# Routed expert tiles: fp16 halves turned one tile later, and router logits with the tokens stationary

## The chip, the core and the metric

One core of a Trainium2 chip runs the whole program. The metric is device time in microseconds (us), median of three runs. Engines: PE is the matrix engine (TensorE; PEld its weight loads), DVE VectorE, ACT ScalarE, POOL GpSimd, SP the engine that only issues transfers.

## The reference

Four layers work in sequence on x (8 x 256 tokens, 512 features): cross attention, a ternary feed-forward layer, linear cross attention, and a mixture of experts. The change touches only the last:

```python
g = x @ sw1.T
u = x @ sw2.T
shared_out = jax.nn.silu(g) * u @ sw3.T                      # 2048 hidden
scores = jax.nn.sigmoid(x @ router_w.T)                      # 8 experts
_, top_idx = jax.lax.top_k(scores + expert_bias, TOPK)       # TOPK = 2
...
h12 = jnp.einsum('td,ehd->teh', flat_x, w12)                 # h1, h2: 256 each
h = jax.nn.silu(h1) * h2
out_e = jnp.einsum('teh,edh->ted', h, w3)
routed_out = jnp.einsum('ted,te->td', out_e, combine)
return shared_out + routed_out
```

## The kernel before

Phases A, B and C are the first three layers; phase D (`phase_d`) is the mixture of experts. Precision comes from fp16 pairs: each fp32 operand is a high fp16 half and a low one (the rest), and a product is three matmuls, high x high, high x low, low x high (helper `three`, lines 140 to 142).

**Shared expert.** Eight chunks of 256 hidden features, four blocks of 512 tokens, two halves of a chunk: 64 steps s. In step s PE does gate(s), up(s), down(s-1), 12 matmuls of 512 columns each. ACT and DVE make SiLU times up (`d_hid`) and its halves (`d_hh`, `d_hl`). Steps 56 to 63, the last chunk, stand behind the routed tiles.

**Router logits.** In steps 1, 3, 5 and 7 `logits(t)` does one block of 512 tokens: the router weights (`r_wT`, 16 columns, high and low halves of 8 experts; `r_wZ`, high and zeros) are stationary and the tokens move, 8 matmuls (L2426, L2427) into 16 partitions of bank 6. ACT copies that to `r_lgT` (L2576), and a step later `logits_turned` turns it back, four fp32 transposes (L2435) into bank 7. DVE's `add_logits` reads the result in step 9.

**Routed tiles.** Tokens are sorted into NT = 39 tiles of 128, each of one expert, whose number stands in `owner`. For tile j:
- POOL gathers the rows of its tokens into `e_x` (L2396, a ring of GR = 3). It waits until both transposes of tile j-3 have landed.
- SP turns both halves by DMA into `e_xTh` and `e_xTl` (L2357, L2358), again a ring of three.
- PE `routed_up(j)`: 12 matmuls of 512 columns, bank 6 or 7. ACT takes SiLU (L2543), DVE multiplies (L2699), into fp32 `d_hid`.
- PE `routed_turn(j)`: two fp32 transposes (L2476) into bank 0 or 1. ACT takes the high half to `d_hh` (L2549), DVE the low one to `d_hl` (L2704).
- PE `routed_down(j)`: 6 matmuls of 512 columns, bank 4 or 5. ACT copies the result to `e_y` (L2555) and SP stores it to `made` (L2361).

PE's order is up(j), down(j-1), turn(j). Before up and before down PE's sequencer loads the expert's number from `owner` into a register (L2457), from which the weights' addresses are made. Behind the last tile come gate(56), down(38), up(56), with waits for the copies of tiles 37 and 38, because banks 4 and 5 serve both.

SP's order, which the change leaves alone, is a single loop:

```python
for j in range(NT + 3):
    if j < NT:
        sp.wait_ge(g_in[j % GR], 16 * (j // GR) + 16)
        if j >= GR:
            sp.wait_ge(e_u, j - GR + 1)
        sp.dma_start_transpose(eTh[:, j % GR], xg[:, j % GR, 0, :])...
        sp.dma_start_transpose(eTl[:, j % GR], xg[:, j % GR, 1, :])...
    if j >= 3:
        sp.wait_ge(e_y, j - 2)
        sp.dma_start(made[(j - 3) * P:(j - 2) * P, :], y[:, (j - 3) % YR, :])...
```

`e_y` at j - 2 means that tiles 0 to j-3 have been copied. So the transposes of tile k are issued behind the store of tile k-4. Afterwards POOL gathers the finished rows back (L2403) and DVE adds them to X (L2681).

Of the kernel before, what the change touches and what calls it, by code (L numbers as in the profile page):

```python
# [15 lines left out]
F32 = mybir.dt.float32  # L16
# [2097 lines left out]
def phase_d(nc, a, env):  # L2114

    sem, bank, X, ident, tg, three = (env[k] for k in ("sem", "bank", "X", "ident", "tg", "three"))
# [3 lines left out]
    def sb(name, shape, dt=F32, stack=None):  # L2120
# [36 lines left out]
    rwZ = sb("r_wZ", [P, KC, 2 * E], F16, rst)  # L2157
    lgT = sb("r_lgT", [2 * E, 2, BLK], F32, rst)
# [31 lines left out]
    w3l = sb("e_w3l", [P, E, KC, HC, P], F16)  # L2190
    y, YR = env["y"], 2
# [7 lines left out]
    r_in, r_wt, r_whi, r_wlo, r_lg, r_lt, r_turn, r_add, r_sig, r_ch, r_cst, r_one, r_msk, r_cnt, r_cut, r_hot, r_used, \  # L2199
        r_who, r_done = (sem("r_" + n) for n in (  # L2200
            "in", "wt", "whi", "wlo", "lg", "ltaken", "turned", "add", "sig", "ch", "const", "ones", "chosen",
# [8 lines left out]
    EUP, EDN, ETH = 6, 4, 0  # L2210
    e_tr = sem("e_turned")
# [47 lines left out]
    def pe_gate(pe, s):  # L2259
        c, t, j = s // SPC, s // JC % BPC, s % JC  # L2260
        if s > 1:
            pe.wait_ge(d_s, s)
        for k in range(KC):
            last = three(bank[GATE][:, :], whs[:, c % 2, 0, k, j * P:(j + 1) * P], wls[:, c % 2, 0, k, j * P:(j + 1) * P],
                         XTh[:, k, t * BLK:(t + 1) * BLK], XTl[:, k, t * BLK:(t + 1) * BLK], k == 0, k == KC - 1)
        last.then_inc(d_g, 1)

    def pe_up(pe, s):
        c, t, j = s // SPC, s // JC % BPC, s % JC
        if s > 1:  # L2270
            pe.wait_ge(d_hm, s)
        for k in range(KC):
            last = three(bank[UP][:, :], whs[:, c % 2, 1, k, j * P:(j + 1) * P], wls[:, c % 2, 1, k, j * P:(j + 1) * P],
                         XTh[:, k, t * BLK:(t + 1) * BLK], XTl[:, k, t * BLK:(t + 1) * BLK], k == 0, k == KC - 1)
        last.then_inc(d_u, 1)
# [15 lines left out]
    def act_step(act, s):  # L2291
        act.wait_ge(d_g, s + 1)
        if s >= 2:
            act.wait_ge(d_lo, s - 1)
        nc.scalar.activation(hid[:, s % 2, :], bank[GATE if s else 0][:, :], ACT.Silu).then_inc(d_s, 1)  # L2295
        act.wait_ge(d_hm, s + 1)
        if s >= 2:
            act.wait_ge(d_dn, s - 1)
        nc.scalar.activation(hh[:, s % 2, :], hid[:, s % 2, :], ACT.Copy).then_inc(d_hi, 1)  # L2299

    def dve_hid(dve, s):
        dve.wait_ge(d_u, s + 1)
        dve.wait_ge(d_s, s + 1)
        nc.vector.tensor_tensor(hid[:, s % 2, :], hid[:, s % 2, :], bank[UP if s else 1][:, :], ALU.mult).then_inc(d_hm, 1)  # L2304
# [22 lines left out]
    with nc.Block() as block:  # L2327
# [80 lines left out]
        def _(pe):  # L2408
# [11 lines left out]
            def logits(t):  # L2420
                pe.wait_ge(r_wlo, 1)
                if t:
                    pe.wait_ge(r_lt, t)
                for k in range(KC):
                    cols = slice(t * BLK, (t + 1) * BLK)
                    nc.tensor.matmul(bank[LG][0:2 * E, :], rwT[:, k, :], XTh[:, k, cols], start=(k == 0), stop=False)  # L2426
                    last = nc.tensor.matmul(bank[LG][0:2 * E, :], rwZ[:, k, :], XTl[:, k, cols], start=False,  # L2427
                                            stop=(k == KC - 1))
                last.then_inc(r_lg, 1)

            def logits_turned(t):
                pe.wait_ge(r_lt, t + 1)
                for i in range(TPB):
                    c = (TILES + t * TPB + i) * 2 * E
                    last = nc.tensor.transpose(bank[TR][:, c:c + 2 * E], lgT[:, t % 2, i * P:(i + 1) * P],  # L2435
                                               ident[0:2 * E, 0:2 * E])
                last.then_inc(r_turn, 1)
# [21 lines left out]
            def routed_up(j):  # L2459
                e = expert(j)  # L2460
                pe.wait_ge(g_tp[j % GR], 32 * (j // GR) + 32)
                if j >= 2:
                    pe.wait_ge(e_m, j - 1)
                for k in range(KC):
                    hi = w12h[:, bass.ds(e, 1), k, :].rearrange("p o c -> p (o c)")
                    lo = w12l[:, bass.ds(e, 1), k, :].rearrange("p o c -> p (o c)")
                    last = three(bank[EUP + j % 2][:, :], eTh[:, j % GR, k, :], eTl[:, j % GR, k, :], hi, lo,
                                 k == 0, k == KC - 1)
                last.then_inc(e_u, 1)

            def routed_turn(j):
                pe.wait_ge(e_m, j + 1)
                if j >= 2:
                    pe.wait_ge(e_lo, j - 1)
                for k in range(HC):
                    last = nc.tensor.transpose(bank[ETH + j % 2][:, k * P:(k + 1) * P], hid[:, j % 2, k * P:(k + 1) * P],  # L2476
                                               ident[:, :])
                last.then_inc(e_tr, 1)

            def routed_down(j):  # L2480
                e = expert(j)
                pe.wait_ge(e_lo, j + 1)
                if j >= 2:
                    pe.wait_ge(e_y, j - 1)
                for k in range(HC):
                    hi = w3h[:, bass.ds(e, 1), :, k, :].rearrange("p o r c -> p (o r) c")
                    lo = w3l[:, bass.ds(e, 1), :, k, :].rearrange("p o r c -> p (o r) c")
                    cols = slice(k * P, (k + 1) * P)
                    last = three(bank[EDN + (j + 1) % 2][:, :].rearrange("p (r c) -> p r c", r=KC), hh[:, j % 2, cols],
                                 hl[:, j % 2, cols], hi, lo, k == 0, k == HC - 1)  # L2490
                last.then_inc(e_dn, 1)

            for s in range(NS * SPC):
                if s == LAST * SPC:
                    pe_down(pe, s - 1)
                    pe.wait_ge(r_done, 2)
                    pieces_turned(pe, NQ - 1)
                    for j in range(NT):
                        routed_up(j)
                        if j:  # L2500
                            routed_down(j - 1)
                        else:
                            pe.wait_ge(d_acc, LAST * BPC)
                        routed_turn(j)
                    pe.wait_ge(e_y, NT - 1)
                    pe_gate(pe, s)
# [19 lines left out]
                if s and s <= SPC and s % JC == 0:  # L2526
                    logits_turned(s // JC - 1)
# [8 lines left out]
        def _(act):  # L2536
            env["ln_normal"](act, "d", B - 1)

            def routed_silu(j):
                act.wait_ge(e_u, j + 1)  # L2540
                if j >= 2:
                    act.wait_ge(e_tr, j - 1)
# [14 lines left out]
            for s in range(NS * SPC):  # L2557
                if s == LAST * SPC:
                    act.wait_ge(d_dn, s)
                    for j in range(NT):  # L2560
                        routed_silu(j)
                        if j:
                            routed_result(j - 1)
                        routed_high(j)
# [6 lines left out]
                if s < SPC and s % JC == JC - 1:  # L2571
                    t = s // JC
                    act.wait_ge(r_lg, t + 1)
                    if t >= 2:
                        act.wait_ge(r_turn, t - 1)
                    nc.scalar.activation(lgT[:, t % 2, :], bank[LG][0:2 * E, :], ACT.Copy).then_inc(r_lt, 1)  # L2576
# [5 lines left out]
        def _(dve):  # L2582
# [4 lines left out]
            def add_logits():  # L2587
                dve.wait_ge(r_turn, BPC)
# [113 lines left out]
            def routed_low(j):  # L2702
                dve.wait_ge(e_hi, j + 1)
                nc.vector.tensor_tensor(hl[:, j % 2, 0:FR], bank[ETH + j % 2][:, 0:FR], hh[:, j % 2, 0:FR],  # L2704
                                        ALU.subtract).then_inc(e_lo, 1)

            def router():
                dve.wait_ge(r_in, 32)
                dve.wait_ge(r_whi, 1)
                link(nc.vector.tensor_tensor(rwT[:, :, E:2 * E], bank[TR][:, 0:KC * E].rearrange("p (k e) -> p k e", k=KC),  # L2710
                                             rwT[:, :, 0:E], ALU.subtract))
                nc.vector.memset(rwZ[:, :, E:2 * E], 0.0)
                nc.vector.tensor_copy(rwZ[:, :, 0:E], rwT[:, :, 0:E]).then_inc(r_wlo, 1)
# [5 lines left out]
            for s in range(NS * SPC):  # L2719
                if s == LAST * SPC:  # L2720
                    dve_result(dve, s // JC - 1)
                    for j in range(NT):
                        routed_mul(j)
                        routed_low(j)
                dve_hid(dve, s)
# [71 lines left out]
```

## Time and profile before

| | us |
|---|---|
| median of three runs (lowest to highest) | 1724.37 (1722.57 to 1724.7) |
| span of the profiled execution | 1722.0 |
| its time over the span | the median less the span is 2.4 |
| first routed up matmul to first matmul of up(56) | 1471.1 to 1655.2 |
| router logits, first to last matmul | 1036.5 to 1092.0 |

The profiled execution's own time is taken as the median, 2.4 us over its span. In a timeline a matmul's length includes the way through the array (0.38 us for 512 columns), while the next begins 0.215 us later; "idle" counts from the end so drawn.

### The profile page before, as it was taken

How to read it: one execution, taken by the hardware profiler on the slowest of the kernel's cores; microseconds unless marked ns; L12 is line 12 of the kernel's file. 1: busy time of each engine (PE TensorE's matmuls, PEld its weight loads, DVE VectorE, ACT ScalarE, POOL GpSimd, SP SyncE). 2: the span in 40 equal slices, each digit the busy share in tenths (PEclk: the TensorE clock that was granted, in tenths of full speed). 3: DMA queues.
4: the chain of work that ended last, by engine and by line, in shares of the span. 5: the costliest groups of instructions: out<-in, count | busy, mean ns of one | idle time of the engine just before them, and what ended most of it. 6: DMA issues, size and time to landing. Idle time of an engine off the chain costs nothing. (4 is left out here: it accounts for less than half of the span.)

```text
span 1722.0 us, 29300 instructions
## 1 busy us (share of the span) xinstructions
PE 1587.8 (92%) x10826; PEld 829.3 (48%) x10826; DVE 973.1 (57%) x1947; ACT 709.2 (41%) x1311; POOL 824.3 (48%) x853
## 2 busy tenths in 40 slices
PE   5769999999877999899999989999999999999998
PEld 3336665665443444345656544444444444444443
DVE  5736666778736999845665543377454333211146
ACT  3268888888855655532232321211111111222221
POOL 3478887877853545443452434344333532112134
PEclk9989999999878999999999999999999999999999
DMA  6745444322333555444554426447454754477746
GB/s 182 160 102 112 99 106 109 93 67 72 92 73 84 110 119 114 93 86 86 96 120 95 78 74 156 110 105 153 92 101 101 154 101 95 109 173 172 168 138 195
DMA packets 453955, 195.68 MB, mean 114 GB/s; under 512 B 395500, under 2 KB 418286, under 8 KB 453816
## 3 DMA queue, kind: packets, MB, share of 16 engines
q1 hardware_dynamic: 448136, 175.19, 46.0%
q0 software_dynamic: 5680, 18.62, 4.1%
q8 instruction: 89, 1.46, 0.4%
q14 instruction: 50, 0.41, 0.1%
HBM read 77.17 MB, written 22.81 MB: 58 GB/s over the span
## 5 line engine op out<-in xcount | busy, mean ns | idle before, releaser
L1109 POOL TENSOR_TENSOR a_pl<-a_prob,a_ph 128x512 f16<-128x512 f32 x256 | 295.2, 1166 | 72.7 <-ACT a_prob L996 72.3
L1199 DVE TENSOR_REDUCE a_mx<-bank 128x2 f32<-128x512 f32 x256 | 173.3, 686 | 97.1 <-PE bank L690 95.5
L140 PE MATMUL bank<-XTh,d_whs 128*128 128x512 f16 x512 | 194.9, 381 | 4.2 <-PEq L89 2.4
L141 PE MATMUL bank<-XTl,d_whs 128*128 128x512 f16 x512 | 194.7, 380 | 0.0
L142 PE MATMUL bank<-XTh,d_wls 128*128 128x512 f16 x512 | 194.6, 380 | 0.0
L995 ACT ACTIVATE a_ph<-bank 128x512 f16<-128x512 f32 x256 | 153.9, 601 | 73.3 <-PE bank L710 35.9
L2384 POOL CAST d_cut<-d_raw 128x512 f16<-128x512 f32 x90 | 56.2, 624 | 227.7 <-DMA d_raw<-in_L_ffn_sw 146.8
L996 ACT ACTIVATE a_prob<-bank 128x512 f32<-128x512 f32 x256 | 154.4, 603 | 0.0
L2304 DVE TENSOR_TENSOR d_hid<-d_hid,bank 128x512 f32<-128x512 f32 x64 | 43.9, 686 | 172.1 <-PE bank L142 168.2
L2295 ACT ACTIVATE d_hid<-bank 128x512 f32<-128x512 f32 x64 | 38.2, 597 | 204.7 <-PE bank L142 204.7
L2299 ACT ACTIVATE d_hh<-d_hid 128x512 f16<-128x512 f32 x64 | 40.3, 630 | 194.7 <-DVE d_hid L2304 194.7
L727 PE MATMUL bank<-a_v,a_ph 128*128 128x17 f16 x1024 | 103.8, 172 | 16.9 <-POOL a_pl L1109 16.9
L2396 POOL DMA_INDIRECT e_x<-rows,d_who x39 | 37.2, 955 | 164.2 <-DMA e_xTl<-e_x 158.1
L2386 POOL TENSOR_TENSOR d_cut<-d_raw,d_cut 128x512 f16<-128x512 f32 x90 | 107.2, 1191 | 7.2
L1502 PE MATMUL bank<-b_wpj,b_hTh 128*128 128x512 f16 x256 | 99.6, 389 | 12.0 <-DMA b_hTl<-b_hcut 12.0
L727 PEld LDWEIGHTS bank<-a_v,a_ph 128*128 128x128 f16 x1024 | 89.0, 97 | 40.1 <-POOL a_pl L1109 18.6
L710 PE MATMUL bank<-a_qT,a_kT 128*128 128x512 f16 x256 | 101.3, 396 | 7.4 <-ACT a_prob L996 7.4
L690 PE MATMUL bank<-a_kT,a_qT 128*128 128x256 f16 x512 | 98.5, 275 | 7.0 <-DVE a_mx L1199 6.6
L2314 DVE SCALAR_TENSOR_TENSOR X<-bank,tg,X 128x512 f32<-128x512 f32 x112 | 76.3, 744 | 49.9 <-PE bank L142 49.9
L731 PE MATMUL bank<-a_v,a_pl 128*128 128x17 f16 x1024 | 102.3, 171 | 0.0
L729 PE MATMUL bank<-a_v,a_ph 128*128 128x16 f16 x1024 | 102.1, 170 | 0.0
L1503 PE MATMUL bank<-b_wpj,b_hTl 128*128 128x512 f16 x256 | 99.4, 388 | 0.0
(349 smaller groups left out, 3996.4 us busy)
## 6 DMA issues: line engine op xcount, KB each, us to landing
d_raw<-in_L_ffn_w SPq DMA_DIRECT2D x48, 256.0 KB, 3.1
d_raw<-in_L_ffn_sw SPq DMA_DIRECT2D x42, 256.0 KB, 3.1
made<-e_y SPq DMA_DIRECT2D x39, 256.0 KB
a_stage<-in_L_ffn_w_fc SPq DMA_DIRECT2D x32, 256.0 KB, 2.9
a_stage<-in_L_ffn_w_proj SPq DMA_DIRECT2D x32, 256.0 KB, 3.1
a_fbuf<-in_ctx SPq DMA_DIRECT2D x16, 256.0 KB, 3.5
rows<-f_cut SPq DMA_DIRECT2D x16, 256.0 KB, 2.5
out_x<-X SPq DMA_DIRECT2D x16, 256.0 KB, 2.4
```

Of the source, the lines that this page charges most:

```text
L140: nc.tensor.matmul(out_ap, lhi, rhi, start=first, stop=False)
L141: nc.tensor.matmul(out_ap, lhi, rlo, start=False, stop=False)
L142: return nc.tensor.matmul(out_ap, llo, rhi, start=False, stop=last_one)
L710: nc.tensor.matmul(bk[:, :], kT[:, par, 2 * g + half, kc * P:(kc + 1) * P], qT[:, par, 2 * g:2 * g + 2, :].rearrange("p r q -> p (r q)"), ...
L727: nc.tensor.matmul(into[:, c:c + HD0 + 1], ph[:, n % NP, q], vv[:, b % 3, kc, g, 0:HD0 + 1], start=first, stop=False, skip_group_check=True)
L729: nc.tensor.matmul(into[:, c:c + HD0], ph[:, n % NP, q], vv[:, b % 3, kc, g, HD0 + 1:VW], start=False, stop=False, skip_group_check=True)
L731: last = nc.tensor.matmul(into[:, c:c + HD0 + 1], pl[:, n % NP, q], vv[:, b % 3, kc, g, 0:HD0 + 1], start=False, stop=(kc == 1), skip_grou ...
L995: nc.scalar.activation(ph[:, n % NP, :], bank[BST + n % 2][:, :], ACT.Exp)
L996: nc.scalar.activation(prob[:, n % 2, :], bank[BST + n % 2][:, :], ACT.Exp).then_inc(ev["E"], 1)
L1109: nc.gpsimd.tensor_tensor(pl[:, n % NP, :], prob[:, n % 2, :], ph[:, n % NP, :], ALU.subtract).then_inc(ev["L"], 1)
L1199: nc.vector.tensor_reduce(mx[:, h, tt, half, 2 * (g % 4):2 * (g % 4) + 2], bank[BS + m % 2][:, :].rearrange("p (r k) -> p r k", r=2), AX_X ...
L2386: nc.gpsimd.tensor_tensor(cut[:, i % RING, 1, :], raw[:, i % RING, :], cut[:, i % RING, 0, :], ALU.subtract).then_inc(p_lo, 1)
```

## The change

Routed tiles: ACT now takes the high half of the product straight from `d_hid` in SBUF to a new fp16 tile `e_hs`, DVE the low half, and PE turns both: four fp16 transposes, high to bank 0 or 1, low to bank 2 or 3, in place of two fp32 ones. ACT and DVE then copy the turned halves to `d_hh` and `d_hl`. PE's order becomes up(j), down(j-2), turn(j-1). The expert's number is loaded once per tile, behind up, and kept for down. Step 56 uses banks 7 and 6 in place of 4 and 5, and the wait for the last copy moves to step 57.

Router: the tokens are stationary (128 of them), the weights move. 16 tiles of 128 tokens times 8 matmuls of 16 or 8 columns, straight into the layout that `add_logits` reads; `r_wZ`, `r_lgT`, ACT's copies and the fp32 transposes go.

```diff
             def logits(t):
-                pe.wait_ge(r_wlo, 1)
-                if t:
-                    pe.wait_ge(r_lt, t)
-                for k in range(KC):
-                    cols = slice(t * BLK, (t + 1) * BLK)
-                    nc.tensor.matmul(bank[LG][0:2 * E, :], rwT[:, k, :], XTh[:, k, cols], start=(k == 0), stop=False)
-                    last = nc.tensor.matmul(bank[LG][0:2 * E, :], rwZ[:, k, :], XTl[:, k, cols], start=False,
-                                            stop=(k == KC - 1))
+                if t == 0:
+                    pe.wait_ge(r_wlo, 1)
+                for n in range(t * TPB, (t + 1) * TPB):
+                    dst = bank[TR][:, (TILES + n) * 2 * E:(TILES + n + 1) * 2 * E]
+                    cols = slice(n * P, (n + 1) * P)
+                    for k in range(KC):
+                        nc.tensor.matmul(dst, XTh[:, k, cols], rwT[:, k, :], start=(k == 0), stop=False)
+                        last = nc.tensor.matmul(dst[:, 0:E], XTl[:, k, cols], rwT[:, k, 0:E], start=False,
+                                                stop=(k == KC - 1))
                 last.then_inc(r_lg, 1)
...
             def routed_turn(j):
-                pe.wait_ge(e_m, j + 1)
+                pe.wait_ge(e_lo, j + 1)
                 if j >= 2:
-                    pe.wait_ge(e_lo, j - 1)
-                for k in range(HC):
-                    last = nc.tensor.transpose(bank[ETH + j % 2][:, k * P:(k + 1) * P], hid[:, j % 2, k * P:(k + 1) * P],
-                                               ident[:, :])
+                    pe.wait_ge(e_th, j - 1)
+                    pe.wait_ge(e_tl, j - 1)
+                for low in range(2):
+                    for k in range(HC):
+                        last = nc.tensor.transpose(bank16(ETH[low] + j % 2)[:, k * P:(k + 1) * P], hs[:, j % 2, low, k * P:(k + 1) * P],
+                                                   ident16[:, :])
                 last.then_inc(e_tr, 1)
...
+                    owners = {0: expert(0)}
                     for j in range(NT):
-                        routed_up(j)
+                        routed_up(j, owners[j])
+                        if j + 1 < NT:
+                            owners[j + 1] = expert(j + 1)
+                        if j >= 2:
+                            routed_down(j - 2, owners[j - 2])
+                        elif j:
+                            pe.wait_ge(d_acc, LAST * BPC)
                         if j:
-                            routed_down(j - 1)
-                        else:
-                            pe.wait_ge(d_acc, LAST * BPC)
-                        routed_turn(j)
-                    pe.wait_ge(e_y, NT - 1)
+                            routed_turn(j - 1)
+                    routed_down(NT - 2, owners[NT - 2])
+                    routed_turn(NT - 1)
+                    pe.wait_ge(e_m, NT)
                     pe_gate(pe, s)
-                    routed_down(NT - 1)
-                    pe.wait_ge(e_y, NT)
+                    routed_down(NT - 1, owners[NT - 1])
                     pe_up(pe, s)
                     continue
+                elif s == EXPERTS + 1:
+                    pe.wait_ge(e_y, NT)
...
             def routed_high(j):
+                act.wait_ge(e_m, j + 1)
+                if j >= 2:
+                    act.wait_ge(e_tr, j - 1)
+                nc.scalar.activation(hs[:, j % 2, 0, :], hid[:, j % 2, 0:FR], ACT.Copy).then_inc(e_hi, 1)
+
+            def take_high(j):
                 act.wait_ge(e_tr, j + 1)
                 if j >= 2:
                     act.wait_ge(e_dn, j - 1)
-                nc.scalar.activation(hh[:, j % 2, 0:FR], bank[ETH + j % 2][:, 0:FR], ACT.Copy).then_inc(e_hi, 1)
+                nc.scalar.activation(hh[:, j % 2, 0:FR], bank16(ETH[0] + j % 2)[:, 0:FR], ACT.Copy).then_inc(e_th, 1)
...
                     for j in range(NT):
                         routed_silu(j)
+                        routed_high(j)
+                        if j >= 2:
+                            routed_result(j - 2)
                         if j:
-                            routed_result(j - 1)
-                        routed_high(j)
+                            take_high(j - 1)
```

On PE in the routed tiles, before, from the end of a down to the next up (`ident,d_hid` is the fp32 transpose, TENSOR_LOAD with its two ISA rows the read of the expert's number, the third ISA the first address):

```order
L142 MATMUL bank5<-e_w3h,d_hl 128x512
L2476 MATMUL bank1<-ident,d_hid 128x128 x2
L2457 TENSOR_LOAD d_owner
L2457 ISA x2
L140 ISA
L140 MATMUL bank6<-e_w12h,e_xTh 128x512
```

The same place after, from the end of up (bank 6) through down (bank 5) to the next up (bank 7); the repeats inside down are the same five rows for the second half:

```order
L142 MATMUL bank6<-e_w12h,e_xTl 128x512
L2452 TENSOR_LOAD d_owner
L2452 ISA x2
L140 ISA
L140 MATMUL bank5<-e_w3h,d_hh 128x512
```

```order
L142 MATMUL bank5<-e_w3h,d_hl 128x512
L2472 MATMUL bank1<-ident16,e_hs 128x128 x2
L2472 MATMUL bank3<-ident16,e_hs 128x128 x2
L140 ISA
L140 MATMUL bank7<-e_w12h,e_xTh 128x512
```

The load has gone from between transposes and up to between up and down, and down is of a tile two back.

On ACT in the routed tiles, before:

```order
L2543 ACTIVATE d_hid<-bank6 128x256
L2555 ACTIVATE e_y<-bank4 128x512
L2549 ACTIVATE d_hh<-bank0 128x256
L2543 ACTIVATE d_hid<-bank7 128x256
L2555 ACTIVATE e_y<-bank5 128x512
```

And after:

```order
L2544 ACTIVATE d_hid<-bank6 128x256
L2550 ACTIVATE e_hs<-d_hid 128x256
L2562 ACTIVATE e_y<-bank5 128x512
L2556 ACTIVATE d_hh<-bank1 128x256
L2544 ACTIVATE d_hid<-bank7 128x256
```

One instruction more per tile stands ahead of the copy to `e_y`, which is now of the tile two behind the SiLU above it.

## Rows read from the trace of the kernel before

**Rows 1.** The page: busy time, share of span, instructions of each engine.
```profile
PE 1587.8 (92%) x10826; PEld 829.3 (48%) x10826; DVE 973.1 (57%) x1947; ACT 709.2 (41%) x1311; POOL 824.3 (48%) x853
```
**Rows 2.** Waits between 1475 and 1655 us: engine, line, releaser; us, times, longest.
```profile
PE bank L140 <- issue: 12.2, 38, 0.6
```
**Rows 3.** Timeline of one routed tile, start us, us, engine; transfers and copies with it.
```profile
1521.96 0.39 PE L140 MATMUL bank<-e_w12h,e_xTh 128*128 x1 [0.35 <-issue]
...
1524.76 0.38 ACT L2543 ACTIVATE d_hid<-bank 128x256 f32<-128x256 f32 x1 [2.46 <-PE bank L142]
...
1525.17 0.42 DVE L2699 TENSOR_TENSOR d_hid<-d_hid,bank 128x256 f32<-128x256 f32 x1 [2.42 <-ACT d_hid L2543]
...
1525.64 0.38 PE L142 MATMUL bank<-e_w3h,d_hl 128*128 x1
...
1525.85 0.38 PE L2476 MATMUL bank<-ident,d_hid 128*128 128x128 f32 x2
1526.05 0.60 ACT L2555 ACTIVATE e_y<-bank 128x512 f32<-128x512 f32 x1 [0.91 <-PE bank L142]
...
1526.51 0.39 PE L140 MATMUL bank<-e_w12h,e_xTh 128*128 x1 [0.27 <-issue]
...
1526.68 0.32 SPq L2361 DMA_DIRECT2D made<-e_y  x1
...
1527.10 1.22 SPq L2357 DMA_TRANSPOSE e_xTh<-e_x  x1
...
1528.36 1.27 SPq L2358 DMA_TRANSPOSE e_xTl<-e_x  x1
```
**Rows 4.** Timeline of PE: first matmul of the first routed up, first of up(56).
```profile
1471.08 0.38 PE L140 MATMUL bank<-e_w12h,e_xTh 128*128 x1
...
1655.22 0.39 PE L140 MATMUL bank<-XTh,d_whs 128*128 128x512 f16 x1 [0.69 <-ACT e_y L2555]
```
**Rows 5.** Transfers writing e_xTl, last line of the tile's view.
```profile
DMA to landing us min/median/max: 2.5/3.7/5.9
```
**Rows 6.** Timeline of SP and POOL: a low transpose, and the gather it releases; then one more gather.
```profile
1475.14 1.27 SPq L2358 DMA_TRANSPOSE e_xTl<-e_x  x1
...
1477.89 0.94 POOL L2396 DMA_INDIRECT e_x<-rows,d_who  x1 [29.74 <-DMA e_xTl<-e_x]
...
1532.30 0.94 POOL L2396 DMA_INDIRECT e_x<-rows,d_who  x1 [3.41 <-DMA e_xTl<-e_x]
```
**Rows 7.** Timeline of PE: logits of one block, and its transposes, with neighbours.
```profile
1036.23 0.38 PE L142 MATMUL bank<-d_whd,d_hl 128*128 128x512 f16 x1
1036.54 0.38 PE L2426 MATMUL bank<-XTh,r_wT 128*16 128x512 f16 x1
...
1038.37 0.39 PE L140 MATMUL bank<-XTh,d_whs 128*128 128x512 f16 x1
...
1045.93 0.38 PE L142 MATMUL bank<-d_whd,d_hl 128*128 128x512 f16 x1
1046.24 0.42 PE L2435 MATMUL bank<-ident,r_lgT 16*128 16x16 f32 x4
1046.59 0.39 PE L140 MATMUL bank<-XTh,d_whs 128*128 128x512 f16 x1
```
**Rows 8.** Phase A: twelve short matmuls with loads between them, first and next matmul.
```profile
111.82 0.17 PE L727 MATMUL bank<-a_v,a_ph 128*128 128x17 f16 x1
...
112.12 0.38 PE L687 MATMUL bank<-a_madd,ident 128*128 128x512 f16 x1
```
**Rows 9.** Phase A by line: weight loads (ns min/median/max), eight fp16 transposes (start, us).
```profile
L727 PEld LDWEIGHTS bank<-a_v,a_ph x1024: 95/96/152, 79.3 to 504.2; 128*128 128x128 f16 x171
...
67.00 0.61 PE L673 MATMUL bank<-ident,a_ks 128*128 128x128 f16 x8
```
**Rows 10.** Stretches: length, busy PE, PEld, DVE, ACT, POOL; granted clock, DMA share, GB/s.
```profile
430.00:473.00 43.00, 35.20 (x447) 21.09 (x445) 33.59 (x64) 36.85 (x72) 37.72 (x36) 0.84 0.36 90
...
1471.00:1655.00 184.00, 169.74 (x794) 80.21 (x791) 35.71 (x82) 48.90 (x117) 31.17 (x33) 1.00 0.65 154
```

More of the change, by code:

```diff
@@ L2114, in phase_d @@
 def phase_d(nc, a, env):
-    sem, bank, X, ident, tg, three = (env[k] for k in ("sem", "bank", "X", "ident", "tg", "three"))
+    sem, bank, bank16, X, ident, ident16, tg, three = (env[k] for k in (
+        "sem", "bank", "bank16", "X", "ident", "ident16", "tg", "three"))
     XTh, XTl, whs, wls, whd, wld, rows = (env[k] for k in ("XTh", "XTl", "whs", "wls", "whd", "wld", "rows"))
@@ L2156, in phase_d @@
     rwT = sb("r_wT", [P, KC, 2 * E], F16, rst)
-    rwZ = sb("r_wZ", [P, KC, 2 * E], F16, rst)
-    lgT = sb("r_lgT", [2 * E, 2, BLK], F32, rst)
     ebias = sb("r_bias", [P, E], F32, rst)
@@ L2190, in phase_d @@
     w3l = sb("e_w3l", [P, E, KC, HC, P], F16)
+    hs = sb("e_hs", [P, 2, 2, FR], F16)
     y, YR = env["y"], 2
@@ L2198, in phase_d @@
     p_hi, p_lo = sem("p_hi"), sem("p_lo")
-    r_in, r_wt, r_whi, r_wlo, r_lg, r_lt, r_turn, r_add, r_sig, r_ch, r_cst, r_one, r_msk, r_cnt, r_cut, r_hot, r_used, \
+    r_in, r_wt, r_whi, r_wlo, r_lg, r_add, r_sig, r_ch, r_cst, r_one, r_msk, r_cnt, r_cut, r_hot, r_used, \
         r_who, r_done = (sem("r_" + n) for n in (
-            "in", "wt", "whi", "wlo", "lg", "ltaken", "turned", "add", "sig", "ch", "const", "ones", "chosen",
+            "in", "wt", "whi", "wlo", "lg", "add", "sig", "ch", "const", "ones", "chosen",
             "counts", "cut", "hot", "used", "who", "done"))
@@ L2209, in phase_d @@
     GATE, UP, LG, TR = 4, 5, 6, 7
-    EUP, EDN, ETH = 6, 4, 0
-    e_tr = sem("e_turned")
+    EUP, EDN, ETH = 6, 4, (0, 2)
+    e_tr, e_th, e_tl = (sem("e_" + n) for n in ("turned", "taken_hi", "taken_lo"))
+    EXPERTS = LAST * SPC
+    GATE_OF, UP_OF = {0: 0, EXPERTS: 7}, {0: 1, EXPERTS: 6}
     ROUND = 12582912.0
@@ L2263, in pe_gate @@
         for k in range(KC):
-            last = three(bank[GATE][:, :], whs[:, c % 2, 0, k, j * P:(j + 1) * P], wls[:, c % 2, 0, k, j * P:(j + 1) * P],
+            last = three(bank[GATE_OF.get(s, GATE)][:, :], whs[:, c % 2, 0, k, j * P:(j + 1) * P], wls[:, c % 2, 0, k, j * P:(j + 1) * P],
                          XTh[:, k, t * BLK:(t + 1) * BLK], XTl[:, k, t * BLK:(t + 1) * BLK], k == 0, k == KC - 1)
@@ L2272, in pe_up @@
         for k in range(KC):
-            last = three(bank[UP][:, :], whs[:, c % 2, 1, k, j * P:(j + 1) * P], wls[:, c % 2, 1, k, j * P:(j + 1) * P],
+            last = three(bank[UP_OF.get(s, UP)][:, :], whs[:, c % 2, 1, k, j * P:(j + 1) * P], wls[:, c % 2, 1, k, j * P:(j + 1) * P],
                          XTh[:, k, t * BLK:(t + 1) * BLK], XTl[:, k, t * BLK:(t + 1) * BLK], k == 0, k == KC - 1)
@@ L2294, in act_step @@
             act.wait_ge(d_lo, s - 1)
-        nc.scalar.activation(hid[:, s % 2, :], bank[GATE if s else 0][:, :], ACT.Silu).then_inc(d_s, 1)
+        nc.scalar.activation(hid[:, s % 2, :], bank[GATE_OF.get(s, GATE)][:, :], ACT.Silu).then_inc(d_s, 1)
         act.wait_ge(d_hm, s + 1)
@@ L2303, in dve_hid @@
         dve.wait_ge(d_s, s + 1)
-        nc.vector.tensor_tensor(hid[:, s % 2, :], hid[:, s % 2, :], bank[UP if s else 1][:, :], ALU.mult).then_inc(d_hm, 1)
+        nc.vector.tensor_tensor(hid[:, s % 2, :], hid[:, s % 2, :], bank[UP_OF.get(s, UP)][:, :], ALU.mult).then_inc(d_hm, 1)
     def dve_low(dve, s):
@@ L2420, in logits @@
             def logits(t):
-                pe.wait_ge(r_wlo, 1)
-                if t:
-                    pe.wait_ge(r_lt, t)
-                for k in range(KC):
-                    cols = slice(t * BLK, (t + 1) * BLK)
-                    nc.tensor.matmul(bank[LG][0:2 * E, :], rwT[:, k, :], XTh[:, k, cols], start=(k == 0), stop=False)
-                    last = nc.tensor.matmul(bank[LG][0:2 * E, :], rwZ[:, k, :], XTl[:, k, cols], start=False,
-                                            stop=(k == KC - 1))
-                last.then_inc(r_lg, 1)
[L2431 to L2437, printed above, removed]
+                if t == 0:
[7 more added lines that the diff above has]
+                                                stop=(k == KC - 1))
+                last.then_inc(r_lg, 1)
             def counts():
@@ L2457, in expert, with routed_up @@
                 return pe.value_load(owner[0:1, j:j + 1], min_val=0, max_val=E - 1)
-            def routed_up(j):
-                e = expert(j)
+            def routed_up(j, e):
                 pe.wait_ge(g_tp[j % GR], 32 * (j // GR) + 32)
@@ L2471, in routed_turn, with routed_down @@
             def routed_turn(j):
-                pe.wait_ge(e_m, j + 1)
+                pe.wait_ge(e_lo, j + 1)
                 if j >= 2:
-                    pe.wait_ge(e_lo, j - 1)
-                for k in range(HC):
-                    last = nc.tensor.transpose(bank[ETH + j % 2][:, k * P:(k + 1) * P], hid[:, j % 2, k * P:(k + 1) * P],
-                                               ident[:, :])
+                    pe.wait_ge(e_th, j - 1)
[4 more added lines that the diff above has]
+                                                   ident16[:, :])
                 last.then_inc(e_tr, 1)
-            def routed_down(j):
-                e = expert(j)
-                pe.wait_ge(e_lo, j + 1)
+            def routed_down(j, e):
+                pe.wait_ge(e_th, j + 1)
+                pe.wait_ge(e_tl, j + 1)
                 if j >= 2:
@@ L2525, in _ @@
                     logits(s // JC)
-                if s and s <= SPC and s % JC == 0:
-                    logits_turned(s // JC - 1)
                 if s == SPC + 6:
@@ L2541, in routed_silu @@
                 if j >= 2:
-                    act.wait_ge(e_tr, j - 1)
+                    act.wait_ge(e_lo, j - 1)
                 nc.scalar.activation(hid[:, j % 2, 0:FR], bank[EUP + j % 2][:, 0:FR], ACT.Silu).then_inc(e_s, 1)
             def routed_high(j):
+                act.wait_ge(e_m, j + 1)
[3 more added lines that the diff above has]
+            def take_high(j):
                 act.wait_ge(e_tr, j + 1)
@@ L2561, in _ @@
                         routed_silu(j)
+                        routed_high(j)
+                        if j >= 2:
+                            routed_result(j - 2)
                         if j:
-                            routed_result(j - 1)
-                        routed_high(j)
+                            take_high(j - 1)
+                    routed_result(NT - 2)
+                    take_high(NT - 1)
                     routed_result(NT - 1)
@@ L2570, in _ @@
                                          ACT.Copy).then_inc(r_whi, 1)
[L2571 to L2576, printed above, removed]
                 if s == SPC + 1:
@@ L2587, in add_logits @@
             def add_logits():
-                dve.wait_ge(r_turn, BPC)
+                dve.wait_ge(r_lg, BPC)
                 lg = bank[TR][:, TILES * 2 * E:2 * TILES * 2 * E].rearrange("p (t e) -> p t e", t=TILES)
@@ L2703, in routed_low, with take_low @@
                 dve.wait_ge(e_hi, j + 1)
-                nc.vector.tensor_tensor(hl[:, j % 2, 0:FR], bank[ETH + j % 2][:, 0:FR], hh[:, j % 2, 0:FR],
+                nc.vector.tensor_tensor(hs[:, j % 2, 1, :], hid[:, j % 2, 0:FR], hs[:, j % 2, 0, :],
                                         ALU.subtract).then_inc(e_lo, 1)
+            def take_low(j):
+                dve.wait_ge(e_tr, j + 1)
+                if j >= 2:
+                    dve.wait_ge(e_dn, j - 1)
+                nc.vector.tensor_copy(hl[:, j % 2, 0:FR], bank16(ETH[1] + j % 2)[:, 0:FR]).then_inc(e_tl, 1)
             def router():
@@ L2709, in router @@
                 dve.wait_ge(r_whi, 1)
[L2710 to L2713, printed above, removed]
+                nc.vector.tensor_tensor(rwT[:, :, E:2 * E], bank[TR][:, 0:KC * E].rearrange("p (k e) -> p k e", k=KC),
+                                        rwT[:, :, 0:E], ALU.subtract).then_inc(r_wlo, 1)
                 dve.wait_ge(r_cst, 1)
@@ L2724, in _ @@
                         routed_low(j)
+                        if j:
+                            take_low(j - 1)
+                    take_low(NT - 1)
                 dve_hid(dve, s)
```

## The prediction, made before the changed kernel ran

> **What bounds the kernel now.** I read the page first: PE is busy 92% of the span [rows 1]. So a change must take time from PE's stream, or it is paid for nothing. Then the timeline of one routed tile [rows 3]: up begins at 1521.96 and the last of 18 wide matmuls at 1525.64, 17 steps of 0.2165 us, so 18 take 3.9. The fp32 transposes follow at 1525.85 without a gap and hold PE for some 0.21 (the pair is drawn 0.38 long, of which 0.17 is the way through the array). The next up comes only at 1526.51, so PE stands 0.66 - 0.21 = 0.45 us. The view of waits calls that "issue", 38 times, 12.2 us (plus 0.17 each that is drawn as busy) [rows 2]. Its place explains it: PE's sequencer stands at the transposes for DVE's product, ready at 1525.17 + 0.42 = 1525.59 [rows 3], and only then reads the next expert's number from memory. The same read ahead of down costs nothing, since PE still has matmuls queued. A tile takes 4.55 us, and the whole stretch from the first up to up(56) 1655.22 - 1471.08 = 184.1 [rows 4].
>
> Last I looked at who feeds the tiles. SP's store of a result starts at 1526.68, the transpose of the high half at 1527.10, of the low one at 1528.36 [rows 3]. No PE wait names a transfer now. The question is how much room there is.
>
> **Routed tiles, PE's own work.** Removed: two fp32 transposes of 0.21 together and the 0.45 stall. Added: four fp16 transposes. Eight of these are drawn 0.61 long in phase A [rows 9]; less 0.17 that is 0.055 each, so four take 0.22, no gain. The read of the number now stands behind up with 12 wide matmuls queued, the place that is free today. If PE alone set the pace, a tile would take 3.9 + 0.22 = 4.1, and 39 tiles plus the 12 matmuls of gate(56), 2.6, take 162.9 in place of 184.1: minus 21.2. That includes the waits at the first tile and around gate(56), for which the change has cover (another up, other banks).
>
> **Routed tiles, the loop through SP.** Count from u(j), the start of up(j). Up and the down behind it run without a gap, the copy to `e_y` starts at 1526.05, so u + 4.09; the store at u + 4.72, the high transpose at u + 5.14, the low one at u + 6.40 [rows 3]. The low one lands a median of 3.7 later [rows 5]. POOL's gather, which waits for that landing, starts 3.94 behind the low transpose of 1528.36 [rows 3, 6]; I take the same 3.9 for PE, landing and wake together. So the transposed tile is ready at 6.4 + 3.9 = 10.3 us past the up that stands before the down whose result was stored.
>
> SP issues the transposes of tile k behind the store of tile k-4. Before, down(k-4) follows up(k-3): tile k is ready at u(k-3) + 10.3 and wanted at u(k-3) + 3 x 4.55 = 13.65, 3.3 us in hand. After, down(k-4) follows up(k-2). Tile k is ready at u(k-2) + 10.3 and wanted two tiles on, at 8.2 by PE's pace, even at today's pace only 9.1. The change spends a whole tile of lead that it doesn't give back at SP. Hence u(k) = u(k-2) + 10.3, 5.15 us a tile.
>
> The sum: up(0), up(1), a turn, then u(2) = 5.4, u(4) = 5.4 + 10.3 = 15.7, and 17 round trips to u(38) = 15.7 + 17 x 10.3 = 190.8. Behind it up, down, turn, down, turn, gate, down: 2.6 + 1.3 + 0.2 + 1.3 + 0.2 + 2.6 + 1.3 = 9.5. Total 200.3 against 184.1, so **plus 16.2**.
>
> Bounds of the landing with its wake: 2.75, the first gather in rows 6 (1475.14 to 1477.89, no other gather in flight); and 4.4, some way over the median toward the 5.9 of rows 5. With 2.75 the loop is 9.15: u(4) = 14.55, u(38) = 170.1, total 179.6, minus 4.5. With 4.4 it is 10.8: 199.8, 209.3, plus 25.2. I take 3.9 because after the change a gather again starts about when a tile's up starts, so beside the next transposes, as in the second case of rows 6.
>
> The Trainium skill, page "DMA: Bandwidth & Descriptors", section "Anatomy of one DMA — SWDGE (gpsimd) path", fits a transfer as about 2.0 us plus bytes over 436 GB/s; as an estimate a 128 KB half would then need 2.3. By that the loop is 8.9 with the wake, and the stretch falls by 9.0. The trace disagrees: the least is 2.5 and the median 3.7 [rows 5].
>
> Engines on the loop: ACT takes the high half ahead of the copy. It can start at 1525.59 + 0.06 and takes between 0.38 (the SiLU of the same 256 columns) and 0.60 (the copy of 512) [rows 3]; with 0.40, near its equal in size, it ends at u + 4.09, just as the copy can start. Taken at nothing; at 0.60 the loop grows by 0.2 and the sum by 3.5. ACT's four instructions sum to under 2 us, DVE's three to 1.3, both within 4.1, and the turned halves are wanted a whole up later, so neither waits.
>
> **Router logits.** One block: from 1036.23 + 0.22 to 1038.37, 1.92; its four fp32 transposes with their edges from 1045.93 + 0.22 to 1046.59, 0.44 [rows 7]. Four blocks: 9.4 us of PE. After: 32 matmuls per block with a full load before each and 16 or 8 columns. Phase A has that shape: twelve in 112.12 - 111.82 = 0.30, 0.025 each [rows 8], although a load is drawn 96 ns long [rows 9]. So 32 x 0.025 + 0.2 for the edges = 1.0 a block, 4.0 in all: **minus 5.4**. Bounds: if a burst of 32 ran at the 0.055 of the fp16 transposes, 7.8, minus 1.6; if each load stood unhidden, 4 x (32 x 0.096 + 0.2) = 13.1, plus 3.7. I take 0.025, the same shape. PE is the chain here, and SP's weight loads wait for PE's downs, so the gain passes on. ACT's four copies, two DVE instructions and a tile of zeros go as well: nothing, since neither engine holds PE there.
>
> The Trainium skill, page "TensorE: Matmul & The Clock Gate", section "LDWEIGHTS (loading the stationary operand)", says that a load takes its columns over 1.2 ns, which speaks against this edit: 107 ns for 128 columns, by estimate 14.5 us for the four blocks, plus 5.1. The trace agrees on the length of one (96) and not that it sets the pace (25).
>
> **Sum.** 16.2 - 5.4 = plus 10.8. The last chunk's own work is unchanged. Up(56) no longer waits for the last copy, 0.69 us plus the 0.17 drawn as busy [rows 4], so POOL's gathers back of the results begin some 0.9 later against PE; that costs between nothing and 0.9, and I take nothing, since a step of the last chunk has 7.8 us of matmuls over DVE's additions. On the median that is 1724.4 + 10.8 = 1735.2.
>
> **Rivals.**
> - *The transposes land sooner* (faster). SP's loop holds, but with a longer tile the gather, store and transposes meet less; DMA share is 0.65 in the stretch [rows 10]. Landing with wake of 2.75 gives minus 4.5 - 5.4, so 1714.5; the total is below the old one while that term is under 3.3. For it: the first case of rows 6. Against: all tiles in a row are fed beside a gather. Between 3.1 and 3.5 the kernel lands within 3.4 us of the old time. The estimate from the Trainium skill's page above would end at 1710.
> - *PE sets the pace after all* (faster). If SP's order doesn't bind, minus 21.2 - 5.4: 1698. Against it stands SP's code order: only a landing and wake under 8.2 - 6.4 = 1.8 allows it, below every row.
> - *Loads set the logits.* Plus 3.7 in place of minus 5.4: 1744.
> - *The clock falls.* PE would be busy 4.1 of 5.15, 80%. In phase A a stretch with 35.2 of 43, 82%, had a granted clock of 0.84 against 1.00 here [rows 10], a mean of time at 2.4 and at 1.2 GHz. At 0.84 up and down take 0.75 more, the loop 11.05: 17 x 0.75 = 12.8 more, 1748.
>
> **How the numbers follow.** Forecast with a landing term of 3.5 to 4.4 (1728 to 1744): 0.58. Loads in the logits 0.04, the clock 0.06. The landing between (within 0.2%, 3.4 us, which is about what a measurement of this kernel can tell from no change): 0.12. Sooner 0.14, PE's pace 0.06. Slower 0.58 + 0.04 + 0.06 = 0.68, same 0.12, faster 0.20. The range leaves out PE's pace, the clock and the far ends of the loads and the landing: 1714 to 1744.
>
> **What would show it.** Right: PE's waits for a transfer into `e_xTh` or `e_xTl` ahead of up, 18 or more times, near 2 us per two tiles; "issue" ahead of up gone; results a mean 5.15 apart; the low transpose starting 6.4 behind an up and that up two before the one it feeds; logits blocks of 1.0. Wrong: results 4.1 apart with no such wait; or low transposes landing within 3.1, or logits matmuls 0.05 to 0.1 apart.

## The result

The changed kernel takes 1733.56 us, median of 16 runs (1725.89 to 1737.99). The kernel before, run beside it, takes 1725.31, median of 16 (1722.40 to 1728.63). The ratio is 1.0046, with a 95% interval of 1.0035 to 1.0057: 8.2 us slower.

| | before | after |
|---|---|---|
| span of the profiled execution | 1722.0 | 1731.2 |
| first logits matmul to first routed up | 434.5 | 427.6 |
| first routed up to first matmul of up(56) | 184.1 | 199.9 |
| up(56) to the end | 66.8 | 66.7 |

Two things moved, in opposite directions: the stretch that holds the logits lost 7 us, the routed tiles gained 15.8. (The first logits matmul itself starts 0.5 us later in this profile, 1037.08 against 1036.54, with nothing changed ahead of it.)

### The profile page after: what moved, and what is told of

Its sections match the earlier page's. It is cut to its first block and busy times, and to the rows that moved or that the text cites. A ratio compares the mean times of both kernels' runs of the same rounds, so it can differ in the third digit from the quotient of the medians.

```text
span 1731.2 us, 29642 instructions
## 1 busy us (share of the span) xinstructions
PE 1588.8 (92%) x10984; PEld 833.6 (48%) x10984; DVE 979.2 (57%) x1984; ACT 723.6 (42%) x1346; POOL 824.4 (48%) x853
```

## The profile after

The page's first part. PE is as busy as in [rows 1], 92%, of a longer span:

```profile
span 1731.2 us, 29642 instructions
## 1 busy us (share of the span) xinstructions
PE 1588.8 (92%) x10984; PEld 833.6 (48%) x10984; DVE 979.2 (57%) x1984; ACT 723.6 (42%) x1346; POOL 824.4 (48%) x853
```

The view of PE's waits over the routed tiles (line, releaser; us, times, longest). It answers to [rows 2]:

```profile
PE bank L140 <- DMA e_xTl<-e_x: 28.8, 29, 2.2
PE bank L140 <- ACT d_hh L2556: 0.8, 1, 0.8
```

"Issue" ahead of up has gone. In its place 29 of the 39 ups wait for the transposed low half. With the 0.17 us per wait that are drawn as busy, that is 28.8 + 29 x 0.17 = 33.7 us, against 12.2 + 38 x 0.17 = 18.7 before.

The timeline of one tile and what it sets going, to be laid beside [rows 3]:

```profile
1505.12 0.39 PE L140 MATMUL bank<-e_w12h,e_xTh 128*128 x1
...
1508.33 0.42 DVE L2704 TENSOR_TENSOR d_hid<-d_hid,bank 128x256 f32<-128x256 f32 x1 [2.88 <-ACT d_hid L2544]
...
1508.79 0.42 ACT L2550 ACTIVATE e_hs<-d_hid 128x256 f16<-128x256 f32 x1 [0.49 <-DVE d_hid L2704]
...
1509.01 0.39 PE L2472 MATMUL bank<-ident,e_hs 128*128 128x128 f16 x4
1509.21 0.60 ACT L2562 ACTIVATE e_y<-bank 128x512 f32<-128x512 f32 x1
...
1509.84 0.32 SPq L2363 DMA_DIRECT2D made<-e_y  x1
1510.25 1.22 SPq L2359 DMA_TRANSPOSE e_xTh<-e_x  x1
...
1510.45 0.39 PE L140 MATMUL bank<-e_w12h,e_xTh 128*128 x1 [1.05 <-DMA e_xTl<-e_x]
...
1511.52 1.27 SPq L2360 DMA_TRANSPOSE e_xTl<-e_x  x1
```

Every distance is the one of before: copy at u + 4.09, store at u + 4.72, high transpose at u + 5.13, low one at u + 6.40. ACT's new instruction (0.42) ends at 1509.21, exactly when the copy can start. The up at 1510.45 waits 1.05 + 0.17 us, and what releases it is its own low transpose, issued 3.34 us earlier, at 1507.11:

```profile
1507.11 1.31 SPq L2360 DMA_TRANSPOSE e_xTl<-e_x  x1
```

The transposes issued at 1510.25 and 1511.52 serve the up after that one. The view of the transfers into `e_xTl` ends, in place of [rows 5], with

```profile
DMA to landing us min/median/max: 2.5/3.5/5.7
```

The stretch of the routed tiles (length, busy PE, PEld, DVE, ACT, POOL, granted clock, DMA share, GB/s), beside [rows 10]:

```profile
1464.50:1666.30 201.80, 171.92 (x881) 82.15 (x880) 43.61 (x121) 65.66 (x157) 31.36 (x33) 0.99 0.59 140
```

The transfer engines are less busy than before (0.59 against 0.65), and yet PE waits for them. That points to a latency and not a rate; e1 tests it.

The mean clock of 0.99 hides one place. Behind a wait of 2.07 us one up ran mostly at the lower of PE's two levels, 1.2 GHz (granted clock 0.50 from 1523 to 1525): it took 5.81 us to the next up in place of 4.11, so 1.7 were lost. Its matmuls are drawn 0.63 long in place of 0.38:

```profile
1521.22 0.39 PE L140 MATMUL bank<-e_w12h,e_xTh 128*128 x1 [2.07 <-DMA e_xTl<-e_x]
...
1523.06 0.63 PE L140 MATMUL bank<-e_w12h,e_xTh 128*128 x1
...
1527.03 0.38 PE L140 MATMUL bank<-e_w12h,e_xTh 128*128 x1
```

The logits of one block, beside [rows 7]:

```profile
1036.87 0.38 PE L142 MATMUL bank<-d_whd,d_hl 128*128 128x512 f16 x1
1037.08 0.17 PE L2429 MATMUL bank<-r_wT,XTh 128*128 128x16 f16 x1
1037.11 0.17 PE L2430 MATMUL bank<-r_wT,XTl 128*128 128x8 f16 x1
...
1037.86 0.17 PE L2430 MATMUL bank<-r_wT,XTl 128*128 128x8 f16 x1
1037.89 0.38 PE L140 MATMUL bank<-XTh,d_whs 128*128 128x512 f16 x1
```

32 matmuls in 0.81 us, 25 ns each, and no edge on either side: 0.81 in place of 1.92 + 0.44.

## The experiments

The theory: the changed kernel is bound by the loop through SP's order, in which transposes of tile k wait for the result of tile k-4, and the change took one tile of lead from it. The rivals: the transfer engines are the bound at any order; the new order on PE or the added work on ACT and DVE costs the time; the stall that the change removes is something other than the read of the expert's number.

| kernel | median us | ratio to the kernel before | 95% interval |
|---|---|---|---|
| changed kernel | 1733.56 | 1.0046 | 1.0035 to 1.0057 |
| e1, changed, SP's store one tile later | 1699.34 | 0.985 | 0.9827 to 0.9873 |
| e2, before, router's part only | 1717.28 | 0.9948 | 0.993 to 0.9966 |
| e3, before, routed part only | 1740.17 | 1.0086 | 1.0067 to 1.0106 |
| e4, before, only the number read once and earlier | 1707.77 | 0.9891 | 0.987 to 0.9913 |
| e5, before, SP's store one tile sooner | 1747.15 | 1.0145 | 1.0117 to 1.0173 |
| e6, before, SP's store one tile later | 1724.78 | 1.0008 | 0.9993 to 1.0022 |
| e7, changed, 36 gathers left out | 1719.38 | 0.9964 | 0.995 to 0.9979 |
| e8, e4 and e2 together | 1700.10 | 0.9861 | 0.9835 to 0.9887 |

The kernel before had a median of 1726.41 beside e1 to e4 (11 runs) and 1724.95 over the 19 runs that e5 to e8 are compared with.

### e1: the lead given back at SP

```diff
-            for j in range(NT + 3):
+            for j in range(NT + 4):
...
-                if j >= 3:
-                    sp.wait_ge(e_y, j - 2)
-                    sp.dma_start(made[(j - 3) * P:(j - 2) * P, :], y[:, (j - 3) % YR, :])...
+                if j >= 4:
+                    sp.wait_ge(e_y, j - 3)
+                    sp.dma_start(made[(j - 4) * P:(j - 3) * P, :], y[:, (j - 4) % YR, :])...
```

> The changed kernel with one edit on SP: the store of tile j-4 instead of j-3 stands behind the transposes of tile j, so that the transposes of tile k wait for the result of tile k-5. Theory (the loop through SP's order bounds the changed kernel): a transposed tile is then ready 10.3 us past an up that stands three tiles ahead, and wanted at 3 x 4.1 = 12.3, so PE's waits for e_xTl vanish, results come 4.1 us apart, the stretch from the first routed up to up(56) falls from 199.9 to about 163 and the time to about 1697. Rival (the transfer engines themselves are the bound, whatever the order): they were busy 65% of 4.55 us, 3.0 us per tile, so at 4.1 they would be near 0.73 to 0.8 with landings of 5 us and more; PE's waits for e_xTl stay and the pace stays over 4.6, time over 1715.

Measured: 1699.34 us, 34 less than the changed kernel. PE's waits in the routed tiles, where the changed kernel has 28.8 us for `e_xTl`:

```profile
PE bank L140 <- DMA e_xTl<-e_x: 1.3, 2, 0.8
PE bank L140 <- ACT d_hh L2556: 0.8, 1, 0.8
```

Results come from 1474.1 to 1630.4:

```profile
L2562 ACT ACTIVATE e_y<-bank x39: 597/597/598, 1474.1 to 1630.4; 128x512 f32<-128x512 f32 x39
```

that is 156.3 over 38 intervals, 4.11 a tile. The first routed up to up(56) takes 165.6, against 199.9 in the changed kernel and about 163 expected. The landing has become longer, not shorter:

```profile
DMA to landing us min/median/max: 2.5/3.9/5.9
```

The transfer engines are busy 0.78 of that stretch, against 0.59 in the changed kernel. So the same transfers at a higher rate, landing later, hold PE only twice once there is a tile of lead. That rules out the transfer engines as the bound of the changed kernel.

### e5 and e6: the same edit on the kernel before, in both directions

```diff
-            for j in range(NT + 3):
+            for j in range(NT + 2):
...
-                if j >= 3:
-                    sp.wait_ge(e_y, j - 2)
-                    sp.dma_start(made[(j - 3) * P:(j - 2) * P, :], y[:, (j - 3) % YR, :])...
+                if j >= 2:
+                    sp.wait_ge(e_y, j - 1)
+                    sp.dma_start(made[(j - 2) * P:(j - 1) * P, :], y[:, (j - 2) % YR, :])...
```

> The kernel before, PE's order untouched, with one edit on SP: the store of tile j-2 instead of j-3 stands behind the transposes of tile j. That takes a tile of lead from the transposes without the change's new order. Theory (the lost lead alone makes the loss): the transposed tile is ready 10.3 us past an up only two tiles ahead, PE waits for e_xTl appear, results come some 5.1 us apart, about plus 16 to plus 20 us, near 1744. Rival (the loss comes from the new order on PE or the extra instructions on ACT and DVE): no wait for e_xTl, time as before within 3 us.

Measured: 1747.15, plus 22.2, somewhat more than the 16 to 20 expected (the profiled execution took 1743.71). PE's matmuls, their order and ACT's and DVE's work are those of the kernel before, and the waits of the changed kernel are there:

```profile
PE bank L140 <- DMA e_xTl<-e_x: 26.9, 30, 2.5
PE bank L140 <- issue: 2.5, 8, 0.4
```

Results run from 1481.2 to 1674.6, 5.09 a tile:

```profile
L2555 ACT ACTIVATE e_y<-bank x39: 597/597/598, 1481.2 to 1674.6; 128x512 f32<-128x512 f32 x39
```

From u(4), the start of up(4), to u(38) there are 17 round trips of 10.26 us, where the changed kernel has 10.27. The pace of the slowed kernels is the same whether the tile of lead is taken on SP or on PE. e5 has neither the new order on PE nor the added work on ACT and DVE, so these don't make the loss. The other direction is e1's edit on the kernel before.

> The kernel before with the SP edit of e1_after_more_lead alone (the store of tile j-4 behind the transposes of tile j). Theory (the kernel before has 3.3 us in hand and isn't bound by SP): within 2 us of the kernel before. Rival (part of the gain of e1_after_more_lead is a gain of SP's order in any kernel): faster by over 5 us.

Measured: 1724.78, ratio 1.0008 with an interval that holds 1, as expected. The kernel before had lead in hand; more of it is worth nothing there. So e1's gain is the removal of a bound that the change had brought.

### e4: what the stall of before was

```diff
-            def routed_up(j):
-                e = expert(j)
+            def routed_up(j, e):
...
-            def routed_down(j):
-                e = expert(j)
+            def routed_down(j, e):
...
+                    owners = {0: expert(0)}
                     for j in range(NT):
-                        routed_up(j)
+                        routed_up(j, owners[j])
+                        if j + 1 < NT:
+                            owners[j + 1] = expert(j + 1)
                         if j:
-                            routed_down(j - 1)
+                            routed_down(j - 1, owners[j - 1])
```

The read that stood ahead of down goes too, as in the change: `routed_down` gets the number that was read for its up.

> The kernel before, where only the read of the next tile's expert number moves from between the transposes and up to between up and down; PE's order of the matmuls, the fp32 transposes and SP's order stay. Theory (the 0.45 us stall at each tile is that read behind a stopped sequencer): PE's issue waits ahead of up shrink from 12.2 us (plus 0.17 each drawn as busy) to a few, a tile takes 4.1 to 4.2 us, and the transposed tile, ready 10.3 us past an up three tiles ahead, is still in time for 12.3: minus 13 to minus 17, about 1710. Rival (the stall is the wait for DVE's product and the restart of the sequencer, not the read): the stall stays over 0.3 and the time falls by less than 5. Second rival (feeding binds at that pace): waits for e_xTl appear.

Measured: 1707.77, minus 18.6 against 1726.41, a little more than expected. The same place as in [rows 3], between the fp32 transposes and the next up:

```profile
1522.23 0.38 PE L142 MATMUL bank<-e_w3h,d_hl 128*128 x1
...
1522.44 0.38 PE L2475 MATMUL bank<-ident,d_hid 128*128 128x128 f32 x2
...
1522.66 0.38 PE L140 MATMUL bank<-e_w12h,e_xTh 128*128 x1
```

Up now starts 0.22 us behind the transposes, not 0.66. There is no "issue" row left among PE's waits. The stall was the read of the number in that place: DVE's product and the fp32 transposes still stand where they stood, and the transposes take their own 0.22 us and no more. 38 times 0.44 is 16.7 of the 18.6. The second rival fails as well: no wait for `e_xTl` appears.

### e2 and e3: the two parts apart

e2 is the kernel before with `logits(t)` and what hangs on it as in the change; e3 has all of the rest of the change.

> The kernel before with the router's part of the change alone. Theory (short matmuls 25 ns apart): four blocks shrink from 9.4 to 3.3 us on PE, minus 6 to minus 7 us, about 1718.5. Rival (part of it is lost again where DVE's router chain holds PE, in the steps behind): minus 3 or less.

> The kernel before with the routed tiles' part of the change alone. Theory: the stretch from the first routed up to up(56) grows from 184.1 to about 200, plus 15 to 16 us, about 1741; together with the router's part alone it adds up to the whole change (plus 8). Rival: the parts don't add, since the router's part shifts the gathers of the first tiles against PE; then the sum of the two misses the whole by over 3 us.

Measured: e2 minus 9.1, e3 plus 13.8 against 1726.41, both 1 to 3 us lower than expected. Together plus 4.6, against plus 8.2 for the whole. The difference of 3.6 is a little more than the rival's 3 us. By the ratios of the table it is 2.1 (plus 5.9 against plus 7.9). But the intervals are 6 us wide for e2 and 7 for e3, so the sum doesn't decide. The profiles say more. In e2 the routed stretch begins at 1467.86 and the first logits matmul stands at 1040.44, so 427.4, where the changed kernel has 427.6. In e3 the last up's first matmul can be told from the last of line 140, 1662.8, against the first, 1472.4: 190.4, where the changed kernel has 1655.9 less 1464.6 = 191.3. Within each stretch the parts add to 1 us; I hold the rest to be scatter between runs, which isn't shown.

### e7: what lengthens a landing

POOL gathers only the first three tiles; the rows of the other 36 are left out, and SP doesn't wait for them (its edit isn't shown):

```diff
                 if j >= GR:
-                    pool.wait_ge(g_tp[j % GR], 32 * (j // GR))
+                    continue
                 pool.indirect_dma_start(xg[:, j % GR, :, :]...
```

> The changed kernel with gathers for the first three tiles only; later tiles turn the rows already in the ring, so 36 gathers of 256 KB are left out and their rows are wrong in the output. Theory (a gather beside the transposes lengthens the landing of the low one from about 2.5 to 3.5 us): the landing of e_xTl falls to 2.5 to 2.8 (median), the loop from 10.0 to 9.1, results come 4.55 to 4.6 apart, minus 15 to minus 20 us against the changed kernel. Rival (the landing is the transposes' own or the store's): median landing stays over 3.3, time within 4 us of the changed kernel.

Measured: 1719.38, 14.2 under the changed kernel, just short of the 15 to 20 expected. The landing fell as expected, the wait only in part:

```profile
DMA to landing us min/median/max: 2.5/2.5/4.0
```

```profile
PE bank L140 <- DMA e_xTl<-e_x: 18.9, 19, 2.4
PE bank L140 <- ACT d_hh L2557: 0.8, 1, 0.8
```

A gather beside the transposes costs 1.0 us of median landing. Many pairs of ups are now 4.1 + 4.8 = 8.9 us long, as 6.4 + 2.5 says. The pace is 4.7 and not 4.5, because every few tiles one takes 5.3 to 6.7. The trace shows what these consist of. Of the 19 ups that waited, 11 started 2.6 us behind their low transpose and 8 started 3.2 to 4.2 behind it. Early in the stretch SP issued two high transposes in 3.0 and 2.7 us in place of 1.2, and one up, behind a wait of 2.40, ran 5.80 us with the clock fallen to 0.51. Why those issues and landings are longer with no gather about is open.

### e8: the number read earlier and the router's part, together

> The kernel before with the read of the expert number moved as in e4_number_ahead and the router's part as in e2_logits_only, with neither fp16 transposes nor the new order of down. Theory: the two add up, minus 18.6 and minus 9, about 1699, as fast as the changed kernel with SP's order mended. Rival (the rest of the change is worth something of its own): the mended changed kernel is faster than this by over 3 us.

Measured: 1700.10, ratio 0.9861. That and e1 (0.985) have intervals that overlap for most of their length; they aren't told apart. Nor are the stretches from the first routed up to up(56): 165.4 in e8, 165.6 in e1. So in the routed tiles the fp16 transposes, the second copy and the new order together bring nothing that these runs can show over reading a register once a tile and earlier. e8's remaining waits name what the new order would still cover:

```profile
PE bank L140 <- ACT e_y L2545: 1.2, 2, 0.7
PE bank L2466 <- DVE d_hid L2683: 1.1, 1, 1.1
```

some 3 us with what is drawn as busy, at the first tile and around gate(56). e1 covers these and has three others (above), 2.1 us and 0.5 drawn as busy.

## Why the prediction was right

Forecast 1735.2 (1714 to 1744) and slower; measured 1733.56, plus 8.2 against a predicted plus 10.8. The mechanism was right, and most of its signs came: 29 waits for `e_xTl`, no "issue" row, the low transpose 6.4 behind the up two before its own. Results are a mean 5.02 apart over all tiles, 5.13 an up from u(4) on. That the routed stretch comes out within 0.4 us of the sum is in part luck: its start was 0.9 us shorter, its landings 2.2 less in sum, its end 1.0 longer, and a fall of the clock added 1.7.

- **The stall at each tile** (0.45 us, the read of the number). Right, shown by e4. The change does remove it.
- **Fp16 for fp32 transposes, no gain.** Right: four are drawn 0.39 long, so 0.22 of PE, as two fp32 ones took 0.21.
- **The loop.** The term that decided the sign. Copy, store and both transposes lie at the offsets taken from the trace of before, to 0.01 us in the tile shown; from tile 4 on the low one stands 6.38 to 6.44 behind its up in 32 of 35. From u(4) = 1479.42 to u(38) = 1653.99 are 174.6 us, 17 round trips of 10.27; the sum had 10.3. One of the 17 holds the up at the lower clock, 1.7 us; without these they come to 10.17 each. The whole stretch came to 199.9 against 200.3. e1, e5 and e6 show the cause from three sides.
- **The landing with its wake, 3.9.** Slightly high: 10.17 less 6.40 is 3.77, wake included, which the long landings hold over their median of 3.5. The gather beside the transposes is in the main why it isn't 2.75, as e7 shows: without gathers the kernel is not slower than before.
- **The start, 15.7.** Too long: u(4) came 14.8 us after u(0), since the first round trip had a landing of 2.6.
- **The end, 9.5, and "neither waits".** Too short: from u(38) to up(56) it is 10.5. Down(37) stands right behind turn(37), with no up between them, and waits 0.8 us, and 0.17 drawn as busy, for ACT's copy of the turned half (the wait on `d_hh` above).
- **ACT's instruction ahead of the copy, taken at nothing.** Right: 0.42 long, and it ends as the copy can start. e5, which doesn't have it, has the same loop.
- **Router logits, minus 5.4.** Right in kind, too small. A block takes 0.81 and not 1.0, since the 0.2 for edges was an error: the short matmuls follow the wide ones with no gap. That is 9.44 - 3.24 = 6.2. The stretch lost 7.0; one wait of PE on `d_hid` a few steps behind the logits (0.4, and 0.17 drawn as busy) has gone besides; it is absent in e1, e2, e7 and e8 too, which have the router's part, and there in e3 to e6, which don't. Some 0.2 is left unexplained.
- **The last chunk, nothing.** Right: 66.8 and 66.7.
- **The rivals.** The sooner landing needed 3.3 or less, and it was 3.77. PE's own pace, 1698, is what e1 reaches with 1699.3, so its price was right and its condition not met. The clock fell once, for one up and 1.7 us, and not to the 0.84 that the rival asked for: 0.99 in the stretch. Loads didn't set the logits: they are drawn 95 ns long and 25 apart. So the rule of the Trainium skill (page "TensorE: Matmul & The Clock Gate", section "LDWEIGHTS (loading the stationary operand)"), that a load takes its columns over 1.2 ns, here 107, is near the length of one and doesn't give the pace. The skill's fit of a transfer on the page "DMA: Bandwidth & Descriptors" (section "Anatomy of one DMA — SWDGE (gpsimd) path"), 2.3 us here by estimate, is made for transfers that GpSimd issues, and SP issues these. It is near the 2.5 that e7 shows with no gather beside them, and far under the 3.5 with one.

## What to carry to other kernels

When a step of a software pipeline moves one iteration later, find every queue whose order was written for the old distance. Here SP's program was untouched, and its store of a result, ahead of the next loads, turned a later down into later loads. Compute the ready time and the wanted time of each transfer before and after; here 3.3 us in hand became a deficit of 2.1 per two tiles. And before rebuilding a pipeline to hide a stall, look for the one instruction in it: the read of a register, moved by a few lines and done once a tile (e4), was worth 18.6 us and took none of the lead from SP's order.

## What the runs showed of the hardware

- A read of a register from memory by PE's sequencer costs 0.44 us of PE when it stands behind a wait that ends just in time, and leaves no gap with 12 wide matmuls queued (before against e4).
- Matmuls of 16 and 8 columns, each with a full load of 128 columns ahead of it, run 25 ns apart in bursts of 32, without a gap to wide ones on either side.
- A transfer's landing depends on what runs beside it: a median of 2.5 us for a 128 KB transpose into `e_xTl` with only the store and the high half (e7), and 3.3 to 3.9 in the nine kernels that have a 256 KB gather beside it (3.5 in the changed kernel, 3.9 in e1). Among these nine no order by pace shows: at 4.1 us a tile it is 3.6 (e8), 3.7 (e4) and 3.9 (e1), and 3.3 and 3.7 at about 4.6 (e6, before).
- Behind a wait of 2.07 us PE's granted clock fell to 0.50 for some 3 us (changed kernel, 1.7 us lost), and behind one of 2.40 to 0.51 (e7). Behind another wait, of 2.17 us at 1563.41 in the changed kernel, it didn't: that up took 4.12.
